# A convolution and a greedy sparse code of 16 images: one coefficient tile in four rebuilt from dictionary rows, and written-out orders for both ends

## The chip, the cores and the metric

One core of one Trainium2 chip runs the kernel. The metric is the device time of one execution in microseconds, the median of the runs.

## The reference

The input `x` is (16, 64, 128, 128), f32. Two layers stand one behind the other, each a residual step on a group norm with 32 groups:

```python
x = x + _L0_conv_ref(_gn(x), L0_conv_weight)
x = x + _L1_conv_ref(_gn(x), L1_conv_dictionary)
```

The first is a circular 3x3 convolution with 64 channels in and out (written with an FFT). The second cuts an image into 4x4 patches over all channels, 1024 numbers each (1024 patches an image), and codes each patch by five greedy steps of orthogonal matching pursuit on a dictionary of 512 normalised words of 1024:

```python
for k in range(1, K_MAX + 1):
    scores = jnp.abs(h * (~mask).astype(h.dtype))
    index = jnp.argmax(scores, axis=1).astype(jnp.int32)
    ...
    x_stack = jax.scipy.linalg.solve_triangular(jnp.swapaxes(L, -1, -2), y, lower=False)[..., 0]
    beta = jnp.einsum('bk,bkn->bn', x_stack, G[I])
    h = h_bar - beta
coeffs = jnp.zeros((B, N), X.dtype).at[bidx[:, None], I].set(x_stack)
```

`G` is the Gram matrix of the words, `h_bar` the correlations of a patch with all 512. The patch that goes out is the dictionary times `coeffs`, a sum of five weighted words.

## The kernel before

**Tiles.** A tile is 128 patches on the partitions (`h`: 512 correlations each). An image has 8, in two groups of T = 4. SyncE loads rows of the image (`xh` for the convolution, `xs` for the statistics) and stores `xa`, the result of the first layer. Per image TensorE does eight rounds of `convolve` (`conv_ps`), eight of `correlate` (16 matmul instructions of 512 columns into one of three banks `gen_ps`, from `z`, the normalised patches, and `dn`, the words), `turn` for each tile and sixteen of `recon`. ScalarE evacuates: `ev` writes `xa`, `z` makes the patches, `h` copies correlations, `ct` copies turned coefficients, `re` copies reconstructed rows to `rb`; `st` and `rt` are the group norm's statistics.

**The pursuit.** A unit (back, g, k) is step k of group g of image i - back. ScalarE writes absolute values (`score`, L625), VectorE finds the largest and its place (`search`, L763 and L772) and the word's index and, for k > 0, the addresses of the cells of the Gram matrix between it and the k words before (`cell`, L781). GpSimd then gathers, one instruction for a cell or a row of each tile: `v` (L476, 4k instructions of 128 numbers) and for k < 4 the word's Gram row (`u`, L489, 4 instructions of 128 rows of 2 KB). VectorE turns the cells into a row of the inverse factor (`factor_row`), orthogonalises the Gram row against the kept ones (`project`, L872) and takes it off `h` (L880). The two groups alternate, so that one's gathers lie beside the other's search: UNITS is the order of the ten units of a period.

**The reconstruction.** After k = 4 `coefficients` (`co`) solves for the five weights `xc`. `ce` builds the dense 128 x 512 coefficients of a tile on VectorE: the first word by one instruction (L668), the other four by a mark `hot` where a count equals the index (L658) and an addition of weight times mark (L674), for two tiles at a time in alternation. `turn` transposes it by four 128x128 matmuls (L926) into `ct`, and `recon` multiplies 4 tiles, 512 columns, by the transposed words `dt`:

```python
for a in range(NA):
    last = pe.matmul(to[:], dt_[:, a, d, :], ct[:, g % CT_RING, a, :], start=(a == 0), stop=(a == NA - 1))
```

Four of these 16 blocks of an image make a quarter in `rb`, of which there are two in turn, and GpSimd adds it to the output in memory (`add`, L497).

**Order.** All engines run in program order. Period i holds the convolution of image i, most of the pursuit of image i - 1, and the reconstruction of image i - 2. VECTOR_PLAN, SCALAR_PLAN and ADD_PLAN say at which point of which unit each piece of other work is put on VectorE, ScalarE and GpSimd; BANKS which of three banks a `correlate` or `recon` uses; `period` of TensorE is written out by hand. The first periods use the same tables with the parts left out whose image doesn't exist; the closing one (i = 16) has tables of its own (TAIL...).

## Time and profile before

| | |
|---|---|
| Median of 3 runs | 3405.57 us (3388.78 to 3411.45) |
| Profiled execution, its own time | 3407.99 us |
| Its span, first to last instruction | 3406.1 us |
| Mean granted TensorE clock | 0.953 |
| TensorE / VectorE / ScalarE / GpSimd busy | 88% / 79% / 50% / 58% |

A period in the middle begins with a search of group 0 of a new image. Busy time of TensorE is near to what it can do only when its granted clock is 1.00, and busy time of GpSimd leaves out the time in which it prepares the next transfer, which the waits list as "issue". The rows that matter follow behind the change.

### The profile page before, as it was taken

What the parts mean: (1) busy time and instruction counts of PE and PEld (TensorE: products, weight loads), DVE (VectorE), ACT (ScalarE), POOL (GpSimd) and SP (SyncE); (2) the same over time, 40 slices, a digit from 0 to 9 for tenths busy, and PEclk for the clock granted to TensorE, in tenths of its full rate; (3) what the DMA queues carried; (4) which work ended last, traced back from release to release, by engine and by line L of the source; (5) the groups of instructions that cost most, each with busy time, mean ns of one, the idle gap of its engine ahead of it and who ended that gap; (6) DMA issues with size and microseconds to landing.
All of it is one profiled execution on the core that took longest, in us unless ns stands there. A gap on an engine that the chain in (4) does not pass through costs nothing.

```text
span 3406.1 us, 33931 instructions
## 1 busy us (share of the span) xinstructions
PE 3012.6 (88%) x9424; PEld 1276.3 (37%) x9424; DVE 2681.5 (79%) x6981; ACT 1717.0 (50%) x2899; POOL 1989.0 (58%) x1869
## 2 busy tenths in 40 slices
PE   4996899899999999999999999999999999995547
PEld 1342334343434444343434434343443434342223
DVE  1137888888888888888888888888888878888883
ACT  4545454564646455464646546464645546442222
POOL 0025576656656666666656556665666676666562
PEclk9997999999999999999999999999999999997778
DMA  3433344443454444344454444445444434432133
GB/s 137 144 115 121 132 133 114 162 126 128 114 164 146 140 130 128 122 126 141 146 157 134 112 146 111 134 140 157 140 113 156 126 121 120 140 106 66 47 74 62
DMA packets 139148, 428.32 MB, mean 126 GB/s; under 512 B 56656, under 2 KB 56912, under 8 KB 121936
## 3 DMA queue, kind: packets, MB, share of 16 engines
q0 software_dynamic: 91776, 204.20, 23.9%
q1 hardware_dynamic: 47184, 221.96, 18.1%
q8 instruction: 76, 1.25, 0.1%
q14 instruction: 112, 0.92, 0.1%
HBM read 289.70 MB, written 136.31 MB: 125 GB/s over the span
## 4 chain that ended last, share of the span: by engine, by line
PE 33%; POOL 23%; DVE 17%; issue 11%; DMA 10%; ACT 4%; ACTq 0%; POOLq 0%; DVEq 0%
POOL v L476 20%; PE gen_ps L967 14%; PE gen_ps L955 10%; DMA u<-marked_rows,chosen 9%; DVE u L872 5%; PE conv_ps L1023 4%; DVE idx L772 4%; DVE top L763 3%; POOL u L489 2%; PE conv_ps L1030 2%; DVE h L880 2%; ACT score L625 1%; DVE ce L674 1%; ACT z L553 1%; PE gen_ps L984 1%
## 5 line engine op out<-in xcount | busy, mean ns | idle before, releaser
L476 POOL DMA_INDIRECT v<-gram_rows,cell x1280 | 1386.3, 1083 | 861.2 <-DVE cell L781 496.8
L955 PE MATMUL gen_ps<-ct,dt 128*128 128x512 f32 x2048 | 943.4, 617 | 67.3 <-ACT rb L541 44.4
L967 PE MATMUL gen_ps<-dn,z 128*128 128x512 f32 x2048 | 915.2, 600 | 27.1 <-ACT z L553 24.0
L1023 PE MATMUL conv_ps<-xh,wc 128*128 128x512 f32 x1536 | 711.0, 613 | 81.1 <-ACT xa L576 80.0
L625 ACT ACTIVATE score<-h 128x512 f32<-128x512 f32 x640 | 379.9, 604 | 726.0 <-DVE top L763 375.8
L489 POOL DMA_INDIRECT u<-marked_rows,chosen x504 | 526.4, 1044 | 230.0 <-issue 149.5
L955 PEld LDWEIGHTS gen_ps<-ct,dt 128*128 128x128 f32 x2048 | 396.9, 198 | 560.5 <-issue 528.9
L967 PEld LDWEIGHTS gen_ps<-dn,z 128*128 128x128 f32 x2048 | 385.7, 192 | 530.9 <-issue 492.0
L872 DVE SCALAR_TENSOR_TENSOR u<-u,nl 128x512 f32<-128x512 f32 x748 | 515.8, 748 | 82.3 <-DMA u<-marked_rows,chosen 79.1
L763 DVE MAX8 top<-score 128x8 f32<-128x512 f32 x640 | 417.7, 690 | 201.8 <-ACT score L625 183.0
L1023 PEld LDWEIGHTS conv_ps<-xh,wc 128*128 128x128 f32 x1536 | 294.1, 195 | 457.9 <-issue 456.8
L772 DVE FIND_INDEX8 idx<-h 128x8 uint32<-128x520 f32 x640 | 432.1, 694 | 0.0
L880 DVE SCALAR_TENSOR_TENSOR h<-u,na,h 128x512 f32<-128x512 f32 x504 | 355.7, 747 | 49.2 <-DMA u<-marked_rows,chosen 48.5
L541 ACT ACTIVATE rb<-gen_ps 128x512 f32<-128x512 f32 x256 | 275.9, 1106 | 223.6 <-PE gen_ps L955 222.0
L674 DVE SCALAR_TENSOR_TENSOR ce<-hot,xc,ce 128x512 f32<-128x512 f16 x512 | 359.3, 741 | 0.0
L1032 PE MATMUL conv_ps<-xh,wq 64*64 64x512 f32 x1536 | 359.2, 597 | 0.0
L1030 PE MATMUL conv_ps<-xh,wq 64*64 64x512 f32 x1536 | 359.2, 597 | 0.0
L553 ACT ACTIVATE z<-xa,fac 128x512 f32<-128x512 f32 x256 | 290.3, 1258 | 39.3 <-PE gen_ps L967 39.3
L576 ACT ACTIVATE xa<-conv_ps,shift 128x1024 f32<-128x1024 f32 x128 | 140.8, 1100 | 278.5 <-PE conv_ps L1032 278.5
L926 PE MATMUL ct_ps<-ident,ce 128*128 128x128 f32 x512 | 85.8, 293 | 143.2 <-DVE ce L674 74.6
L1030 PEld LDWEIGHTS conv_ps<-xh,wq 64*64 64x64 f32 x1536 | 102.0, 131 | 238.4 <-issue 238.4
L530 ACT ACTIVATE ct<-ct_ps 128x512 f32<-128x512 f32 x128 | 76.2, 595 | 196.3 <-PE ct_ps L926 196.3
(110 smaller groups left out, 1819.3 us busy)
## 6 DMA issues: line engine op xcount, KB each, us to landing
xh<-x_paired SPq DMA_DIRECT2D x128, 650.0 KB, 4.9
y_rows<-xa SPq DMA_DIRECT2D x64, 1024.0 KB, 5.2
y_rows<-rb POOLq DMA_DIRECT2D x64, 1024.0 KB, 8.8
xs<-x_pairs SPq DMA_DIRECT2D x120, 512.0 KB, 3.8
v<-gram_rows,cell POOLq DMA_INDIRECT x1280, 2.4
u<-marked_rows,chosen POOLq DMA_INDIRECT x504, 4.5
xa<-x_pairs SPq DMA_DIRECT2D x4, 1024.0 KB, 7.9
dn<-atoms SPq DMA_DIRECT2D x1, 2048.0 KB, 11.6
```

What stands on the lines that cost most here:

```text
L476: pool.indirect_dma_start(v[:, g, k - 1, j, t:t + 1], None, cells, bass.IndirectOffsetOnAxis(ap=cell[:, g, k // (KMAX - 1), j, t:t + 1], a ...
L489: pool.indirect_dma_start(kept(img, g, k, t), None, marked, bass.IndirectOffsetOnAxis(ap=chosen[:, g, t:t + 1], axis=0))\
L625: act.activation(score[t % 2][:], h[:, g * T + t, 0:ATOMS], ACT.Abs).then_inc(score_ready[g], 1)
L674: dve.scalar_tensor_tensor(ce[:, place, :], hot[:, m % HOT_RING, :], coef, ce[:, place, :], ALU.mult, ALU.add).then_inc(ce_step, 1)
L763: dve.max(top8[:, t, :], score[t % 2][:]).then_inc(top_found[g], 1)
L772: dve.max_index(idx8[:, t, :], h[:, g * T + t, ATOMS:HW], h[:, g * T + t, :]).then_inc(located[g], 1)
L872: dve.scalar_tensor_tensor(kept(img, g, k, t), kept(img, g, j, t), nl[:, g, k - 1, j, t:t + 1], kept(img, g, k, t), ALU.mult, ALU.add).the ...
L880: dve.scalar_tensor_tensor(hh, kept(img, g, k, t), na[:, g, k, t:t + 1], hh, ALU.mult, ALU.add)\
L955: last = pe.matmul(to[:], dt_[:, a, d, :], ct[:, g % CT_RING, a, :], start=(a == 0), stop=(a == NA - 1))
L967: last = pe.matmul(to[:], z[:, t % 2, d // PATCH, d % PATCH, :], dn[:, d, :], start=(d == 0), stop=(d == ND - 1))
L1023: pe.matmul(conv_ps[:, a], wc[:, tap, a * CIN:a * CIN + P], rows[:, a + 1:a + 2 * CP:2, tap:tap + W], start=(tap == 0), stop=False)
L1030: pe.matmul(conv_ps[above, a], wq[second, tap, :], rows[second, a:a + 2 * CP - 1:2, tap:tap + W], start=False, stop=(tap == TAPS - 1))
```

## The change

1. **Three tiles in four are multiplied (TURNED = 3).** `ce`, `turn` and `ct` leave the fourth tile out; `recon` has 384 columns in place of 512. For the fourth tile, `fetch` gathers the five chosen words themselves, 128 rows of 4 KB each, from a new table in memory (`atom_rows`, written once by SyncE from `dt` after image 1). ScalarE scales the first by its weight (`ps`), VectorE adds the other four (`pk`, 1024 columns each), and TensorE transposes a 128x128 part of the sum into the last 128 columns of each block's bank. Two buffers hold the sums, two the fetched words, so a fetch of word 3 or 4 waits for the addition two before it. `coefficients` ends with a copy of the indices (`pick`).
2. **One outgoing buffer (RB_RING = 1)** in place of two: the first `re` of each quarter waits until the quarter before has been added in memory.
3. **Orders.** The first three images and the last two have an order of their own on every engine (HEAD, TAIL with 18 and 32 units; with the 11 periods between them, 160 units as before). In the middle, group 1's coefficients and reconstruction come a period later (image i - 3); weights and indices of four images are kept (CO_RING). The loads of `xs` are spread over more rounds.
4. **The last group of the last image** reads its cells on the chip for k > 1 (`read_cells`): VectorE multiplies a mark with the kept rows and sums; GpSimd gathers only the first cell of each tile, and the elimination in `factor_row` falls away.

The core of the diff:

```diff
+HEAD_IMAGES = 3
+TAIL_IMAGES = 2
+CO_RING = 4
...
-CE_RING = 4
+TURNED = T - 1
+CE_RING = TURNED
+ROWS_RING = 4
 XS_RING = 2
-RB_RING = 2
+RB_RING = 1
...
-    0: [0, 1, 2], 5: [3, 4], 7: [5, 6, 7],
+    0: [0, 1], 1: [2], 2: [3, 4, 5], 3: [6], 5: [7],
...
+HEAD = ((3, 0, 0), (3, 0, 1), (3, 0, 2), (3, 1, 0), (3, 0, 3), (3, 1, 1), (3, 0, 4), (3, 1, 2), (2, 0, 0), (3, 1, 3),
...
+TAIL = ((3, 0, 0), (4, 1, 3), (3, 0, 1), (4, 1, 4), (3, 0, 2), (3, 1, 0), (3, 0, 3), (3, 1, 1), (3, 0, 4), (3, 1, 2),
...
+VECTOR_PLAN = {
+    1: [(3, ("ce", 1, 0))], 1.5: [(2, ("co", 0))], 11.5: [(3, ("pk", 1, 3)), (3, ("pk", 1, 4)), (3, ("ce", 1, 1))],
+    21: [(2, ("ce", 0, 0))], 24: [(2, ("pk", 0, 1)), (2, ("pk", 0, 2))],
...
+ADD_PLAN = {
+    0: [(3, ("get", 1, 4)), (2, ("get", 0, 0))], 2: [(2, ("get", 0, 1)), (2, ("get", 0, 2))],
+    5: [(3, ("add", 1, 0)), (2, ("get", 0, 3)), (2, ("get", 0, 4))], 6: [(3, ("add", 1, 1)), (2, ("get", 1, 0))],
+    7: [(2, ("get", 1, 1)), (2, ("add", 0, 0)), (2, ("get", 1, 2))], 9: [(2, ("get", 1, 3)), (2, ("add", 0, 1))],
+}
...
+                if i == 1:
+                    sp.wait_ge(turned_copied, 2 * NA)
+                    sp.dma_start(words.rearrange("(a p) (d c) -> p a d c", p=P, c=P), dt_[:]).then_inc(rows_out, 16)
...
-                        for j in range(k):
+                        for j in range(1 if read_in_place(img, g, k) else k):
...
+            def fetch(img, g, j):
+
+                n = img * GROUPS + g
+                if j == 0:
+                    pool.wait_ge(pick_ready, n + 1)
+                    if n == 0:
+                        pool.wait_ge(rows_out, 16)
+                    if n > 1:
+                        pool.wait_ge(recon_done, (n - 1) * ND)
+                elif n > 0 or j > 2:
+                    pool.wait_ge(atom_step, n * (KMAX - 1) + j - 2)
+                place, _ = atom_load(n, j)
+                pool.indirect_dma_start(atom[:, place, :], None, words,
+                                        bass.IndirectOffsetOnAxis(ap=pick[:, img % CO_RING, g, j:j + 1], axis=0))\
+                    .then_inc(atom_loaded[place], 16)
...
+                elif kind == "ps":
+
+                    g, = a
+                    n = img * GROUPS + g
+                    act.wait_ge(solve_step, solved(img, g))
+                    act.wait_ge(atom_loaded[n % 2], 16 * atom_load(n, 0)[1])
+                    act.activation(atom[:, n % 2, :], atom[:, n % 2, :], ACT.Copy,
+                                   scale=xc[:, img % CO_RING, g, 0, TURNED:T]).then_inc(atom_scaled, 1)
...
+                    members = (0, 1) if pair == 0 else (2,)
...
+                elif kind == "pk":
+
+                    g, j = a
+                    n = img * GROUPS + g
+                    own = n % 2
+                    other, loads = atom_load(n, j)
+                    dve.wait_ge(atom_loaded[other], 16 * loads)
+                    if j == 1:
+                        dve.wait_ge(atom_scaled, n + 1)
+                    else:
+                        dve.wait_ge(atom_step, n * (KMAX - 1) + j - 1)
+                    dve.scalar_tensor_tensor(atom[:, own, :], atom[:, other, :], xc[:, img % CO_RING, g, j, TURNED:T],
+                                             atom[:, own, :], ALU.mult, ALU.add).then_inc(atom_step, 1)
...
+            def read_cells(img, g, k):
+
+                dve.wait_ge(which_ready[g], at(img, KMAX, k + 1))
+                dve.wait_ge(row_step[g], at(img, ROWS, T * sum(range(k))))
+                for j in range(1, k):
+                    for t in range(T):
+                        m = T * sum(range(1, k - 1)) + (j - 1) * T + t
+                        if m:
+                            dve.wait_ge(cell_read, m)
+                        dve.scalar_tensor_tensor(hot[:, 0, :], count[:], which[:, img % CO_RING, g, k, t:t + 1],
+                                                 kept(img, g, j, t), ALU.is_equal, ALU.mult,
+                                                 accum_out=v[:, g, k - 1, j, t:t + 1]).then_inc(cell_read, 1)
+                dve.wait_ge(cell_read, T * sum(range(1, k)))
...
+            def recon(img, g, d):
+
+                pe.wait_ge(ct_ready, at(img, GROUPS * TURNED, (g + 1) * TURNED))
+                if d == 0:
+                    pe.wait_ge(atom_step, (img * GROUPS + g + 1) * (KMAX - 1))
+                m = bank_of(img, images, ("re", g, d))
+                room(m, recon_out, at(img, GROUPS * ND, g * ND + d + 1))
+                to = gen_ps[m]
                 for a in range(NA):
-                    last = pe.matmul(to[:], dt_[:, a, d, :], ct[:, g % CT_RING, a, :], start=(a == 0), stop=(a == NA - 1))
...
+                    pe.matmul(to[:, 0:TURNED * P], dt_[:, a, d, :], ct[:, g % CT_RING, a, :], start=(a == 0), stop=(a == NA - 1))
+                own = (img * GROUPS + g) % 2
+                pe.transpose(to[:, TURNED * P:], atom[:, own, d * P:(d + 1) * P], ident[:]).then_inc(recon_done, 1)
```

TensorE, a whole period in the middle, from the last blocks of one group's reconstruction to the first correlations of the image (L955/L1178 are `recon`, L1180 the new transposes, L926/L1160 `turn`, L967/L1192 `correlate`; x counts equal instructions in a row). Before:

```order
L955 MATMUL gen_ps<-ct,dt 128x512 x12
L926 MATMUL ct_ps<-ident,ce 128x128 x4
L955 MATMUL gen_ps<-ct,dt 128x512 x4
L1004 MATMUL conv_ps<-mv,avg 128x5
L926 MATMUL ct_ps<-ident,ce 128x128 x8
L955 MATMUL gen_ps<-ct,dt 128x512 x16
L967 MATMUL gen_ps<-dn,z 128x512 x8
L955 MATMUL gen_ps<-ct,dt 128x512 x4
L967 MATMUL gen_ps<-dn,z 128x512 x8
L1004 MATMUL conv_ps<-mv,avg 128x5
```

In the change:

```order
L1229 MATMUL conv_ps<-mv,avg 128x5
L1160 MATMUL ct_ps<-ident,ce 128x128 x4
L1229 MATMUL conv_ps<-mv,avg 128x5
L1178 MATMUL gen_ps<-ct,dt 128x384 x4
L1180 MATMUL gen_ps<-ident,atom 128x128
L1178 MATMUL gen_ps<-ct,dt 128x384 x4
L1180 MATMUL gen_ps<-ident,atom 128x128
L1178 MATMUL gen_ps<-ct,dt 128x384 x4
L1180 MATMUL gen_ps<-ident,atom 128x128
L1234 MATMUL conv_ps<-fac,tap_sum 128x1
L1178 MATMUL gen_ps<-ct,dt 128x384 x4
L1180 MATMUL gen_ps<-ident,atom 128x128
```

A block is now four matmuls (two instructions each) of 384 columns and one transpose; the averages of the group norm move ahead of the reconstruction's second half.

GpSimd, from the gathers of the last two units of a period to those of the fourth and fifth of the next (`v` are cells, `u` Gram rows, `atom` the fetched words, `y_rows` the additions). Before:

```order
L476 DMA v<-gram_rows,cell 128x1 x24
L489 DMA u<-marked_rows,chosen 128x512 x4
L497 DMA y_rows<-rb 128x2048 x2
L489 DMA u<-marked_rows,chosen 128x512 x4
L476 DMA v<-gram_rows,cell 128x1 x12
L489 DMA u<-marked_rows,chosen 128x512 x4
L476 DMA v<-gram_rows,cell 128x1 x4
L489 DMA u<-marked_rows,chosen 128x512 x4
L476 DMA v<-gram_rows,cell 128x1 x24
```

In the change:

```order
L660 DMA v<-gram_rows,cell 128x1 x24
L673 DMA u<-marked_rows,chosen 128x512 x4
L696 DMA atom<-atom_rows,pick 128x1024
L681 DMA y_rows<-rb 128x2048
L673 DMA u<-marked_rows,chosen 128x512 x4
L696 DMA atom<-atom_rows,pick 128x1024 x2
L660 DMA v<-gram_rows,cell 128x1 x12
L673 DMA u<-marked_rows,chosen 128x512 x4
L660 DMA v<-gram_rows,cell 128x1 x4
L673 DMA u<-marked_rows,chosen 128x512 x4
L696 DMA atom<-atom_rows,pick 128x1024 x2
L660 DMA v<-gram_rows,cell 128x1 x24
```

Five of a period's ten fetches stand here, each between one unit's gathers and the next one's; the additions stand apart.

VectorE, the end of the program, between the last search and the last solve (`ce` and `hot` belong to group 0, `tmp_last` to `sq_last` to the last solve of group 1). Before, behind nine rows of group 0's tiles:

```order
L658 TENSOR_SCALAR hot<-count,which 128x512 x2
L674 SCALAR_TENSOR_TENSOR ce<-hot,xc,ce 128x512 x2
L794 TENSOR_TENSOR tmp_last<-nl,v 128x12
L797 TENSOR_TENSOR v<-v,tmp_last 128x12
L794 TENSOR_TENSOR tmp_last<-nl,v 128x8
L797 TENSOR_TENSOR v<-v,tmp_last 128x8
L794 TENSOR_TENSOR tmp_last<-nl,v 128x4
L797 TENSOR_TENSOR v<-v,tmp_last 128x4
L801 SCALAR_TENSOR_TENSOR nl<-v,rd 128x16
L805 TENSOR_TENSOR sq_last<-nl,v 128x16
```

In the change:

```order
L996 SCALAR_TENSOR_TENSOR cell<-which 128x16
L1000 SCALAR_TENSOR_TENSOR hsel<-pos,top 128x4
L889 SCALAR_TENSOR_TENSOR atom<-atom,xc 128x1024 x2
L1013 SCALAR_TENSOR_TENSOR hot,v<-count,which,u 128x512 x4
L1013 SCALAR_TENSOR_TENSOR hot,v<-count,which,xs 128x512 x4
L1013 SCALAR_TENSOR_TENSOR hot,v<-count,which,xh 128x512 x4
L1030 SCALAR_TENSOR_TENSOR nl<-v,rd 128x16
L1034 TENSOR_TENSOR sq_last<-nl,v 128x16
L1038 TENSOR_REDUCE ss_last<-sq_last 128x4
```

Twelve reads on the chip stand in place of the six steps of elimination, and no tile of group 0 is left behind the last search.

## Rows read from the trace of the kernel before

**Rows 1.** The page: shares (1) and 40 slices (2)
```profile
PE 3012.6 (88%) x9424; PEld 1276.3 (37%) x9424; DVE 2681.5 (79%) x6981; ACT 1717.0 (50%) x2899; POOL 1989.0 (58%) x1869
...
PE   4996899899999999999999999999999999995547
...
DVE  1137888888888888888888888888888878888883
```

**Rows 2.** Timeline, VectorE: start us, us, line, operation, tiles [idle before]
```profile
550.35 1.30 DVE L763 MAX8 top<-score 128x8 f32<-128x512 f32 x2 [0.54 <-ACT score L625]
...
3098.56 1.30 DVE L763 MAX8 top<-score 128x8 f32<-128x512 f32 x2 [0.83 <-ACT score L625]
```

**Rows 3.** Windows: us; busy PE, PEld, DVE, ACT, POOL (count); clock; DMA share, GB/s
```profile
178.90:550.40 371.50, 318.64 (x1038) 134.07 (x1037) 269.86 (x713) 192.04 (x337) 204.70 (x194) 0.93 0.38 121
550.40:2703.20 2152.80, 2029.23 (x6404) 858.10 (x6403) 1827.17 (x4775) 1170.41 (x1981) 1367.65 (x1277) 0.98 0.45 135
2703.20:3098.60 395.40, 371.09 (x1162) 156.73 (x1160) 329.47 (x858) 192.26 (x315) 258.60 (x234) 0.97 0.41 120
3098.60:3273.60 175.00, 77.80 (x180) 35.07 (x180) 160.43 (x399) 49.06 (x72) 107.34 (x108) 0.74 0.30 75
3273.60:3364.20 90.60, 55.03 (x130) 25.25 (x131) 65.41 (x176) 19.10 (x24) 42.89 (x44) 0.77 0.24 47
3364.20:3406.10 41.90, 28.75 (x72) 12.64 (x70) 0.04 (x1) 10.86 (x11) 2.53 (x3) 0.89 0.42 75
```

**Rows 4.** Groups by line, 550.4 to 2703.2: count, busy us, mean ns, idle before
```profile
L955 PE MATMUL gen_ps<-ct,dt 128*128 128x512 f32 x1408 | 646.5, 615 | 48.3 <-ACT rb L541 33.3 <-ACT ct L530 15.1
...
L926 PE MATMUL ct_ps<-ident,ce 128*128 128x128 f32 x352 | 56.2, 283 | 18.9 <-DVE ce L674 10.4 <-ACT ct L530 8.6
...
L872 DVE SCALAR_TENSOR_TENSOR u<-u,nl 128x512 f32<-128x512 f32 x528 | 364.2, 748 | 57.2 <-DMA u<-marked_rows,chosen 54.8
...
L674 DVE SCALAR_TENSOR_TENSOR ce<-hot,xc,ce 128x512 f32<-128x512 f16 x352 | 247.0, 741 | 0.0
L658 DVE TENSOR_SCALAR hot<-count,which 128x512 f16<-128x512 f16 x352 | 108.4, 348 | 0.0
L668 DVE TENSOR_SCALAR ce<-count,which,xc 128x512 f32<-128x512 f16 x88 | 46.0, 565 | 0.4
...
L785 DVE SCALAR_TENSOR_TENSOR hsel<-pos,top 128x4 f32<-128x4 f32 x110 | 18.1, 165 | 0.8
...
L476 POOL DMA_INDIRECT v<-gram_rows,cell x880 | 962.5, 1094 | 559.4 <-DVE cell L781 308.6 <-issue 250.8
L489 POOL DMA_INDIRECT u<-marked_rows,chosen x353 | 362.5, 1027 | 135.5 <-issue 105.1 <-DVE chosen L777 30.4
```

**Rows 5.** Waits, 550.4 to 2703.2: us in total, times, longest
```profile
DVE top L763 <- ACT score L625: 107.2, 59, 5.2
...
POOL y_rows L497 <- ACT rb L541: 90.6, 11, 9.7
...
DVE tmp L794 <- DMA v<-gram_rows,cell: 50.6, 13, 5.0
...
DVE h L880 <- DMA u<-marked_rows,chosen: 27.7, 26, 2.5
...
DVE tmp_last L794 <- DMA v<-gram_rows,cell: 16.6, 19, 2.4
```

**Rows 6.** The page, DMA issues: count, KB each, us to landing
```profile
y_rows<-rb POOLq DMA_DIRECT2D x64, 1024.0 KB, 8.8
...
v<-gram_rows,cell POOLq DMA_INDIRECT x1280, 2.4
u<-marked_rows,chosen POOLq DMA_INDIRECT x504, 4.5
```

**Rows 7.** Timeline of the end, TensorE, VectorE
```profile
3366.68 27.73 PE L955 MATMUL gen_ps<-ct,dt 128*128 128x512 f32 x64 [0.69 <-ACT ct L530]
...
3343.23 0.17 DVE L794 TENSOR_TENSOR tmp_last<-nl,v 128x12 f32<-128x12 f32 x1 [13.58 <-DMA v<-gram_rows,cell]
```

More of the change, by code:

```diff
@@ L169, in units, with bank_of @@
-def units(i, images):
-    return TAIL if i == images else UNITS
-def planned(plan, tail, last, place):
-    return tail.get(place, ()) if last else [(lag(what), what) for what in plan.get(place, ())]
-def bank_of(back, what, last):
-    return [((back, what) if last else what) in bank for bank in (TAIL_BANKS if last else BANKS)].index(True)
+)
+def bank_of(img, images, what):
+    if img < images and any((HEAD_IMAGES - img, what) in bank for bank in HEAD_BANKS):
+        return [(HEAD_IMAGES - img, what) in bank for bank in HEAD_BANKS].index(True)
+    if any((images - img, what) in bank for bank in TAIL_BANKS):
+        return [(images - img, what) in bank for bank in TAIL_BANKS].index(True)
+    return [what in bank for bank in BANKS].index(True)
@@ L498, in add, with period @@
                     .then_inc(recon_added[(g * PHASES + ph) % RB_RING], 16)
[L500 to L506 removed]
+            def fetch(img, g, j):
[12 more added lines that the diff above has]
+                    .then_inc(atom_loaded[place], 16)
+            def period(i, order, plan):
+                for n, (back, g, k) in enumerate(order):
+                    gather(i - back, g, k)
+                    for b, (kind, *what) in plan.get(n, ()):
+                        if kind == "add":
                             add(i - b, *what)
+                        else:
+                            fetch(i - b, *what)
             for a in range(NA):
@@ L603, in root, with period @@
                 act.activation(gs[:, 2:3], gs[:, 1:2], ACT.Sqrt, bias=eps[:, 0:1]).then_inc(gn_root[n], 1)
-            def period(i, par):
-                here = parts(i)
-                for n, (back, g, k) in enumerate(units(i, images)):
+            def period(i, order, plan):
+                for b, what in plan.get(-1, ()):
+                    extra(what, i - b)
+                for n, (back, g, k) in enumerate(order):
                     img = i - back
-                    if here[back]:
-                        scored.append((img, g, k))
+                    scored.append((img, g, k))
@@ L949, in recon, with room @@
[L949 to L960 removed]
+            def room(m, taken, count):
+                if m in free:
+                    pe.wait_ge(*free[m])
+                free[m] = (taken, count)
```

702 lines of the change are left out of this document (417 added, 285 removed), and 163 rows, old and new, of tables (BANKS, HEAD_SCALAR_PLAN, HEAD_VECTOR_PLAN, SCALAR_PLAN).

## The prediction

> **What bounds the kernel now.** I read the page's engine shares first, then its slices [rows 1]. TensorE is busy 88% of the span, VectorE 79%, GpSimd 58%; TensorE's slices are nearly all 9 from the third to the thirty-sixth, but open with 4 and close with 5547. VectorE's slices are the reverse: 1, 1, 3 at the start and 8 until the last. So the run has three parts, and I cut it where VectorE begins its first search (178.88), the first search of period 3 (550.35), of period 14 (2703.18) and of the closing period 16 (3098.56); two of these starts stand in [rows 2], the others are read in the same way. The stretches between them give the table on which everything below rests [rows 3]: a start of 178.9, a head of 371.5, eleven whole periods in 2152.8 (195.7 each), and a tail of 702.9 us.
>
> In one of the eleven periods TensorE is busy 2029.23 / 11 = 184.5 us (94%) and VectorE 1827.17 / 11 = 166.1 (85%). GpSimd's busy time is 1367.65 / 11 = 124.3, but its queue takes more: before most gathers come 0.3 us of "issue" in which it can do nothing else, 250.8 + 105.1 us in all [rows 4], so the queue is taken (1367.65 + 355.9) / 11 = 156.7 us (80%). TensorE is the bound here. VectorE idles 29.6 us a period; its largest named waits [rows 4, 5] are for scores, 107.2 / 11 = 9.7 us (ScalarE, which stands in its queue behind evacuations of matmuls), and for gathered rows and cells, (54.8 + 50.6 + 27.7 + 16.6) / 11 = 13.6.
>
> From 3098.6 to 3273.6 ten units are searched with TensorE only 44% busy; VectorE is busy 160.43 of 175.0 us, 92% [rows 3]. That stretch shows how close VectorE comes to its own floor with this order of units when TensorE doesn't hold it, and it is my measure for the changed kernel.
>
> **The change part by part: one period.** TensorE: the 128 matmul instructions of the reconstruction go from 512 to 384 columns. They are busy 646.5 / 11 = 58.8 us a period [rows 4], so a quarter less is -14.7. Two of eight tiles are no longer turned: 8 transposes at 56.2 / 352 = 0.16 are -1.3. Sixteen transposes of a word are new, +2.6 at the same 0.16. Net -13.4, TensorE 171.1. That time follows columns down to 384 is not shown here; the turns take 0.16 at 128 columns, a quarter of the width and 35% of the 0.459 (646.5 / 1408) of a 512-column one, so the saving on a quarter lies between 0.22 x 58.8 = 12.7 and 14.7. I take the upper, since the busy time of a turn holds the filling of a lone group of four, which a long row of blocks pays once.
>
> VectorE: a coefficient tile costs 4 x (247.0 + 108.4) / 352 + 46.0 / 88 = 4.56 us [rows 4]; two fewer are -9.1. Eight additions of 1024 columns are new. No row has this shape. One of 512 columns lasts 748 ns and one of 4 columns 165 [rows 4], a slope of 1.15 ns a column, so 748 + 512 x 1.15 = 1.34 us each; bounds are 1.2 (twice the 0.69 busy of one, less a shared start) and 1.5 (twice 748). That is +10.7. Two copies of the picked indices are +0.3. The third tile now stands alone, so its marks and additions no longer alternate with a partner's: eight steps with some 0.15 of uncovered latency, +1.2, bounds 0 and 3. Net +3.1, VectorE 169.
>
> GpSimd: ten fetches of 512 KB. A row gather is busy 362.5 / 353 = 1.03 us and comes with 0.3 of issue [rows 4], so +13.3, and the queue is taken 170 us. Their landing: a gather of cells lands 2.4 us after its issue, one of 256 KB after 4.5 [rows 6], so by the slope 512 KB after 6.6; bounds 4.5 and 9. What is queued behind a fetch is the next gather, for which VectorE waits; the queue idles (308.6 + 30.4) / 11 = 31 us a period for VectorE's indices [rows 4], and that idle time takes most of the ten.
>
> The Trainium skill, "DMA: Bandwidth & Descriptors", section on the anatomy of one DMA on the SWDGE path, gives 2.0 us plus the bytes at 436 GB/s, which would be 3.2 us for 512 KB. The trace disagrees at 256 KB: 4.5 us against 2.6 by the page. By its figure the fetches would be cheaper, and no term of the sum would change.
>
> ScalarE: one scaling of 1024 columns per group for one copy of 512, about +1 us on an engine 54% busy. Nothing. A single buffer for the outgoing rows is a new wait: the next quarter's first copy waits for the previous addition to land, 8.8 us after its issue [rows 6], and behind that copy stand the scores. I give it no term of its own beyond the share taken below, since the copies of two quarters now have a whole search between them in the plan; see the rivals for what it costs uncovered.
>
> The sum of a period: the floors are TensorE 171, VectorE 169, GpSimd 170. None alone fills 9 parts in 10 of the present 195.7. VectorE needs 169 / 0.92 = 184 at the share it reaches unhindered; at its present 85% it would need 199. With TensorE freed but two other queues fuller I take 90%, so 188. Eleven periods: 11 x (195.7 - 188) = -85, between 11 x 11.7 = -129 and about -10.
>
> TensorE's clock: the granted clock is 0.98 in the periods at 94% busy, 0.93 in the head at 86%, 0.74 at 44% [rows 3]. At 171 of 188 (91%) I expect about 0.96, which makes 171 into 175: still under 188, so nothing.
>
> The Trainium skill, "TensorE: Matmul & The Clock Gate", Part 1, says that the clock is halved when the array has been idle and given back when it has been busy, which speaks against any saving on TensorE. These rows agree with its direction; it costs nothing as long as TensorE isn't the last to finish.
>
> **The head.** It is written out on its own now, and the second group's coefficient tiles of the first image leave it. VectorE's 269.9 us lose 8 tiles (36.5) and get 3 tiles and 6 additions (13.7 + 8.0): 255. TensorE loses half of a reconstruction. Its share now is 73%, since in the first units one group alone goes from search to gather to search. I take 77.5%: 329 us, -42; bounds -15 and -65.
>
> **The tail.** VectorE is busy 329.47 + 160.43 + 65.41 = 555.3 us from 2703.2 to 3364.2 (84%) [rows 3]. Added: 4 images x 3.1 = 12; the delayed group's 3 tiles and 2 additions, 16.4; and 24 reads of cells on the chip at 364.2 / 528 = 0.69, 16.6, less a dozen tiny operations (2). About 598. What the reads remove: the last solve waits 13.58 us for sixteen gathers [rows 7], and twelve reads (8.3) with four gathers beside them take their place; that shows in the share. With the conv work spread over the tail's whole length I take 90%: 664 against 661, +3. Then the last eight blocks: 27.73 us of matmuls [rows 7] become 20.8 + 1.3, -5.6; but the last word's fetches go through two buffers, so I add 3 for the fourth and fifth. The tail comes to 0; bounds -40 and +30.
>
> Sum against the profiled execution's own 3408.0 (span 3406.1; the median of the runs is 3405.6, so both agree to 0.1%): -85 - 42 + 0 = -127, **3281 us**.
>
> **The rivals.** First, the pursuit's chain through GpSimd is already the floor. For it: 13.6 us of waits for gathered data a period although TensorE bounds, a queue 80% taken, and gathers of one group that take up to (962.5 + 250.8) / 880 x 16 = 22 us [rows 4] in front of the other group's. Against it: the 175 us stretch, with the same order of units and 14.6 us of idle VectorE in all [rows 3]. Then ten fetches cost their 13 us and a period comes to 194; head -30: 3408 - 19 - 30 = 3359. 
>
> Second, it goes better: the separate orders for the ends and the deeper lag keep VectorE at 92% everywhere. Period 184, head 315, tail -25: 3408 - 129 - 56 - 25 = 3198.
>
> Third, slower: the single outgoing buffer. Four times a period ScalarE can stand for the addition's issue and 8.8 us of landing, some 40 us; TensorE's three banks fill behind it and VectorE's scores stand behind it. It is uncovered when the copy of the next quarter comes less than 10 us after the last one's. Every microsecond exposed costs 11 on the total; from 11.5 a period all of the gain is gone, and with 15 exposed (37%) a period is 203: 3408 + 80 - 42 + 4 = 3450. For it: GpSimd already waits 90.6 us in the eleven periods until a quarter is copied, with two buffers [rows 5]. Against it: ScalarE is idle 46% of the time, and the four additions are spread over the period.
>
> **Chances.** Forecast 0.50; gather chain 0.18; better 0.22; single buffer 0.10. A measurement of this kernel can tell about 1%, 34 us. The forecast and the better case are faster by more; of the gather chain 0.09 is and the rest within 1%; of the single buffer 0.08 is slower. Faster 0.81, same 0.11, slower 0.08. The range: from the better case's 3198 to a little over the gather chain's 3359, 3195 to 3380; below it 0.08 is left, above 0.12.
>
> **What would show it.** Periods between searches of 184 to 192 us; the reconstruction's instructions at 0.75 of their busy time; additions of 1024 columns at 1.2 to 1.5 us; the ends of VectorE's and TensorE's shares near 90%. Wrong: VectorE waiting over 20 us a period for gathers (first rival), or ScalarE or TensorE waiting over 10 us a period for an outgoing copy (third); a head over 355 us, or a tail over 730.

## The result, and the profile after

The changed kernel takes 3287.77 us, the median of 4 runs (3283.51 to 3298.51), against 3404.97 us (3388.78 to 3411.45) for the kernel before: a ratio of 0.967, 95% interval 0.963 to 0.971. The forecast was 3281. The profiled execution took 3298.51 us by its own time, with a span of 3296.2. Below, ratios and intervals leave out executions in a slower state of the chip; one of an experiment's own runs was such a one, in experiment 11, where the median without it is 3303.09 us.

Cut at the same searches as [rows 3], the windows of the changed kernel (columns as there: stretch, its length, busy time of TensorE, its weight loads, VectorE, ScalarE and GpSimd, granted clock, DMA share, GB/s) are:

```profile
0.00:178.40 178.40, 131.49 (x442) 53.93 (x442) 28.94 (x64) 85.62 (x165) 5.28 (x13) 1.00 0.37 134
178.40:513.40 335.00, 287.62 (x969) 123.10 (x970) 257.17 (x677) 182.62 (x324) 199.36 (x195) 0.93 0.45 149
513.40:2577.00 2063.60, 1897.75 (x6495) 868.35 (x6494) 1858.49 (x4697) 1178.15 (x1981) 1417.23 (x1390) 0.97 0.57 169
2577.00:3212.00 635.00, 458.76 (x1484) 219.26 (x1482) 549.74 (x1365) 258.43 (x403) 426.55 (x394) 0.86 0.46 130
3212.00:3258.30 46.30, 31.86 (x94) 18.10 (x93) 39.26 (x92) 15.61 (x18) 14.91 (x12) 0.85 0.56 132
3258.30:3296.20 37.90, 22.29 (x74) 12.65 (x72) 0.00 (x0) 9.03 (x9) 2.71 (x3) 0.90 0.46 83
```

The head went from 371.5 to 335.0 us (-36.5), the eleven periods from 2152.8 to 2063.6 (-89.2; 187.6 each, where they were 195.7), and the tail from 702.9 to 719.2 (+16.3). With -0.5 at the start that is -109.9 on the span. In a period TensorE is now busy 1897.75 / 11 = 172.5 us (92%) and VectorE 1858.49 / 11 = 169.0 (90%).

The groups by line, in the eleven periods, that answer to [rows 4] (L1178 is `recon`, L1180 the turn of the word's sum, L889 the addition, L696 the fetch):

```profile
L1178 PE MATMUL gen_ps<-ct,dt 128*128 128x384 f32 x1408 | 509.2, 510 | 21.9 <-ACT rb L749 20.6
L889 DVE SCALAR_TENSOR_TENSOR atom<-atom,xc 128x1024 f32<-128x1024 f32 x88 | 112.7, 1280 | 2.8 <-DVE atom L889 0.5
L696 POOL DMA_INDIRECT atom<-atom_rows,pick x110 | 111.1, 1010 | 33.5 <-issue 33.5
L1180 PE MATMUL gen_ps<-ident,atom 128*128 128x128 f32 x176 | 48.0, 273 | 0.0
```

The reconstruction's busy time is 509.2 where it was 646.5, -12.5 us a period: 0.79 of it, for 0.75 of the columns. This ratio and the 48.0 us of the turns must be read with care, because the records of neighbouring instructions of TensorE overlap. The timeline of two blocks shows the distance from start to start:

```profile
1005.42 2.75 PE L1178 MATMUL gen_ps<-ct,dt 128*128 128x384 f32 x8
1008.00 0.27 PE L1180 MATMUL gen_ps<-ident,atom 128*128 128x128 f32 x1
1008.11 2.75 PE L1178 MATMUL gen_ps<-ct,dt 128*128 128x384 f32 x8
```

Eight instructions of 384 columns take 1008.00 - 1005.42 = 2.58 us, 0.32 each, and the turn takes 0.11 until the next block starts, though its record is 0.27 long. The 64 instructions of 512 columns in 27.73 us [rows 7] come to 0.43 each. By this measure the time does follow the columns (0.32 / 0.43 = 0.75), and sixteen turns put back some 1.8 us a period and not 48.0 / 11 = 4.4. All products into `gen_ps` together, correlations and turns included, are busy 1128.45 us in the eleven periods where they were 1263.18, -12.2 a period.

And the waits of the same stretch, which answer to [rows 5] (columns: engine, what waits, what ended the wait, us in total, times, longest):

```profile
ACT rb L749 <- DMA y_rows<-rb: 140.7, 21, 9.6
DVE top L978 <- ACT score L830: 93.2, 67, 3.4
PE conv_ps L1229 <- DVE fac L912: 61.6, 11, 7.2
POOL y_rows L681 <- ACT rb L749: 39.8, 20, 4.4
PE conv_ps L1248 <- DMA xh<-x_paired: 37.4, 11, 5.2
DVE h L1116 <- DMA u<-marked_rows,chosen: 21.2, 12, 2.8
DVE tmp L1023 <- DMA v<-gram_rows,cell: 13.7, 10, 2.4
DVE u L1108 <- DMA u<-marked_rows,chosen: 6.9, 10, 2.2
DVE tmp_last L1023 <- DMA v<-gram_rows,cell: 3.1, 4, 1.3
```

VectorE's waits for gathered data are (21.2 + 13.7 + 6.9 + 3.1) / 11 = 4.1 us a period, a third of what they were, though ten larger transfers now pass through the same queue. New are ScalarE's wait for the outgoing buffer, 140.7 / 11 = 12.8, and two waits of TensorE: 5.6 for VectorE's step of the statistics and 3.4 for the convolution's rows. They look like the next things to remove. Experiments 8, 10 and 12 tried the two of TensorE, and it brought nothing.

### The profile page after: what moved, and what is told of

The parts are those of the page before. It is cut to its first block, busy times and chain, and to the rows that moved or that the text cites. A ratio compares the mean times of both kernels' runs of the same rounds, so it can differ in the third digit from the quotient of the medians.

```text
span 3296.2 us, 34238 instructions
## 1 busy us (share of the span) xinstructions
PE 2829.8 (86%) x9552; PEld 1295.4 (39%) x9552; DVE 2733.6 (83%) x6889; ACT 1729.5 (52%) x2899; POOL 2066.0 (63%) x2005
## 4 chain that ended last, share of the span: by engine, by line
PE 28%; DVE 22%; POOL 21%; DMA 11%; issue 11%; ACT 5%; SPq 0%; ACTq 0%; POOLq 0%; DVEq 0%
POOL v L660 18%; PE gen_ps L1192 11%; PE gen_ps L1178 7%; DVE u L1108 6%; PE conv_ps L1248 5%; DVE idx L987 5%; DMA y_rows<-rb 4%; DMA u<-marked_rows,chosen 4%; DVE top L978 3%; POOL u L673 3%; DVE h L1116 2%; PE conv_ps L1255 2%; DMA xh<-x_paired 2%; ACT score L830 2%; DMA v<-gram_rows,cell 1%
## 5 line engine op out<-in xcount | busy, mean ns | idle before, releaser
L660 POOL DMA_INDIRECT v<-gram_rows,cell x1256 | 1307.8, 1041 | 706.5 <-issue 362.1
L1192 PE MATMUL gen_ps<-dn,z 128*128 128x512 f32 x2048 | 912.8, 600 | 28.4 <-ACT z L761 23.1
L1178 PE MATMUL gen_ps<-ct,dt 128*128 128x384 f32 x2048 | 751.8, 516 | 100.1 <-ACT rb L749 80.0
L1248 PE MATMUL conv_ps<-xh,wc 128*128 128x512 f32 x1536 | 720.7, 620 | 106.1 <-ACT xa L783 64.1
L673 POOL DMA_INDIRECT u<-marked_rows,chosen x504 | 515.3, 1022 | 186.1 <-issue 153.2
L1192 PEld LDWEIGHTS gen_ps<-dn,z 128*128 128x128 f32 x2048 | 384.3, 192 | 514.6 <-issue 488.1
L1178 PEld LDWEIGHTS gen_ps<-ct,dt 128*128 128x128 f32 x2048 | 395.5, 202 | 394.6 <-issue 202.4
L876 DVE SCALAR_TENSOR_TENSOR ce<-hot,xc,ce 128x512 f32<-128x512 f16 x384 | 275.9, 744 | 4.5
L696 POOL DMA_INDIRECT atom<-atom_rows,pick x160 | 165.0, 1031 | 91.4 <-issue 46.0
L889 DVE SCALAR_TENSOR_TENSOR atom<-atom,xc 128x1024 f32<-128x1024 f32 x128 | 163.8, 1280 | 13.6 <-DMA atom<-atom_rows,pick 9.7
```

The source lines that it names most:

```text
L660: pool.indirect_dma_start(v[:, g, k - 1, j, t:t + 1], None, cells, bass.IndirectOffsetOnAxis(ap=cell[:, g, k // (KMAX - 1), j, t:t + 1], a ...
L673: pool.indirect_dma_start(kept(img, g, k, t), None, marked, bass.IndirectOffsetOnAxis(ap=chosen[:, g, t:t + 1], axis=0))\
L1178: pe.matmul(to[:, 0:TURNED * P], dt_[:, a, d, :], ct[:, g % CT_RING, a, :], start=(a == 0), stop=(a == NA - 1))
L1192: last = pe.matmul(to[:], z[:, t % 2, d // PATCH, d % PATCH, :], dn[:, d, :], start=(d == 0), stop=(d == ND - 1))
L1248: pe.matmul(conv_ps[:, a], wc[:, tap, a * CIN:a * CIN + P], rows[:, a + 1:a + 2 * CP:2, tap:tap + W], start=(tap == 0), stop=False)
```

## The experiments

The first four ran on a chip on which the kernel before took 4018 us, the others on chips on which it took 3399 to 3409. So every result is given by its ratio to the kernel before, run beside it on the same chip (the changed kernel has 0.967), and stretches are compared among the traces of the second kind alone. "Head", "period" and "tail" are cut as above.

**Experiments 1 and 5: the orders alone.** All four tiles are multiplied again, in the changed kernel's orders and with its one outgoing buffer; fetches, scaling, additions and the turn of the sum are gone.

```diff
-TURNED = T - 1
+TURNED = T
-                    members = (0, 1) if pair == 0 else (2,)
+                    members = (0, 1) if pair == 0 else (2, 3)
...
-                    pe.matmul(to[:, 0:TURNED * P], dt_[:, a, d, :], ct[:, g % CT_RING, a, :], start=(a == 0), stop=(a == NA - 1))
+                    last = pe.matmul(to[:], dt_[:, a, d, :], ct[:, g % CT_RING, a, :], start=(a == 0), stop=(a == NA - 1))
```

> The changed kernel's orders (its plans, its own orders for head and tail, its bank tables, its last cells read on chip, one outgoing buffer), but all four tiles multiplied, so no dictionary rows fetched, scaled, added or turned. My theory, that the rebuilt tile carries most of the gain in the middle (TensorE's own work per period 184.5 -> 172.5) and the orders most of the gain in the head: TensorE's work is back at about 185 a period, the period at 193 to 196, the time 3340 to 3390. Rival, that the orders carry it all: period 188 to 190, time 3290 to 3315, and the rebuilt tile is worth nothing. Second rival, that the single outgoing buffer costs in this order: period over 197, time over 3400.

Measured on the first chip: 4201.54 us, 1.044 of before (1.039 to 1.049).

> The same kernel as the first experiment (the changed kernel's orders, four tiles multiplied, one outgoing buffer), run again, because the kernel before itself took 4018 us on the chip of those runs and 3405 on the chip of the first comparison. My theory, that the rebuilt tile carries the gain of the middle and the orders that of the head: on a chip where the kernel before takes about 3405, a period of 193 to 196 and 3340 to 3390 us in all. Rival, that the orders carry it all: period 188 to 190, 3290 to 3315 us. Second rival, the single outgoing buffer: period over 197, over 3400 us.

Measured: 3434.83 us, 1.010 (1.0085 to 1.0118). Its windows, with the end of VectorE's work as the last cut:

```profile
178.21:511.42 333.21, 292.42 (x963) 122.23 (x964) 253.61 (x678) 181.31 (x323) 195.10 (x186) 0.93 0.39 130
511.42:2694.70 2183.28, 2026.89 (x6404) 860.09 (x6403) 1837.68 (x4794) 1175.42 (x1981) 1320.29 (x1279) 0.97 0.46 133
2694.70:3372.02 677.32, 521.80 (x1527) 226.14 (x1525) 579.95 (x1485) 269.71 (x419) 385.99 (x366) 0.90 0.37 98
```

The head is 333.2, as short as in the changed kernel, so the head's gain of 37 belongs to the orders. The period is 198.5: 2.8 longer than before, with TensorE at 184.3. From here to the changed kernel the period falls by 10.9, with 11.8 us less work for TensorE and 1.9 us more for VectorE. The tail (677.3 + 53.5) is 730.8, 28 longer than before. So orders, single buffer and the reads on the chip together cost 1%, and the rebuilt tile, put into these orders, is worth 1 - 0.967 / 1.010 = 4.3%. The rebuilt tile in the old orders wasn't run. The period was over my range and the total was where the rival of the single buffer had it, though this run doesn't say that the buffer is the reason.

**Experiment 2: two buffers in the new orders.**

```diff
-RB_RING = 1
+RB_RING = 2
```

(on experiment 1, whose memory has room for it; the changed kernel's has not).

> As the run before it (the changed kernel's orders, four tiles multiplied), with two outgoing buffers again. It prices the single buffer in the new orders. My theory: the wait for the outgoing transfer (12.8 us a period on ScalarE in the changed kernel) hides behind ScalarE's free time, so within 10 us of the run with one buffer. Rival, that it is paid in part: 20 to 60 us faster than with one buffer (2 to 5 us a period).

Measured: 4212.22 us, 1.047 (1.042 to 1.051), the same as with one. In the new orders the second buffer is worth nothing there. This was seen on the first chip alone, where a period of either kernel is near 256 us and not 198.5, so it doesn't show that the second buffer would be worth nothing on the others.

**Experiments 3 and 9: one buffer in the old orders.** The kernel before with `RB_RING = 1` for 2.

> The kernel before with one outgoing buffer in place of two and nothing else. My theory as in the prediction: the wait on ScalarE is below what it has to spare, so 0 to +25 us (0 to 2 a period), 3405 to 3430. Rival of the prediction (the buffer as the bound): more than 11.5 us a period uncovered, so over 3500 us.

Measured on the first chip: 4727.34 us, 1.174 (1.168 to 1.180).

> The kernel before with one outgoing buffer instead of two, run again on another chip than at first (there the kernel before took 4018 us and this one 4727). My theory as in the prediction: below what ScalarE has to spare, 3405 to 3430. Rival 3 of the prediction: over 11.5 us a period uncovered, over 3530.

Measured: 4112.27 us, 1.209 (1.204 to 1.215). My theory is wrong by some 700 us and the prediction's rival right, for this order. The timeline of ScalarE (start, length, line, tile, idle time before it and what ended it) shows the wait, and GpSimd's shows its cause:

```profile
1502.23 1.07 ACT L541 ACTIVATE rb<-gen_ps 128x512 f32<-128x512 f32 x1
...
1553.02 1.07 ACT L541 ACTIVATE rb<-gen_ps 128x512 f32<-128x512 f32 x1 [31.53 <-DMA y_rows<-rb]
```

and on GpSimd:

```profile
1508.83 1.05 POOL L476 DMA_INDIRECT v<-gram_rows,cell  x1 [24.22 <-DVE cell L781]
1510.19 1.00 POOL L476 DMA_INDIRECT v<-gram_rows,cell  x1 [0.30 <-issue]
...
1543.24 0.96 POOL L489 DMA_INDIRECT u<-marked_rows,chosen  x1 [0.30 <-issue]
1544.20 1.05 POOL L497 DMA_DIRECT2D y_rows<-rb  x1
...
1567.98 0.90 POOL L497 DMA_DIRECT2D y_rows<-rb  x1 [22.73 <-ACT rb L541]
```

The quarter was complete at 1503.3. Its addition stood behind 28 gathers in GpSimd's order and was issued at 1544.2, 41 us later; it landed 8.8 us after that, and only then could ScalarE go on. Then GpSimd stood at the next addition for 22.73 us until the next quarter was copied, with the gathers behind it. So ScalarE and GpSimd wait for each other in turn. In the changed kernel the same pair of views shows on ScalarE:

```profile
1019.08 1.96 ACT L749 ACTIVATE rb<-gen_ps 128x512 f32<-128x512 f32 x2
1032.96 3.00 ACT L749 ACTIVATE rb<-gen_ps 128x512 f32<-128x512 f32 x3 [9.06 <-DMA y_rows<-rb]
```

and on GpSimd:

```profile
1023.73 1.02 POOL L681 DMA_DIRECT2D y_rows<-rb  x1
1039.31 1.00 POOL L681 DMA_DIRECT2D y_rows<-rb  x1 [1.43 <-ACT rb L749]
```

Complete at 1021.0, issued at 1023.7, landed 9.2 us later. With one buffer in both, the delay before the issue is 41 us here and 2.7 there, so the price of a single buffer seems to go with the place of the addition. This is read from two traces: no run moved the additions alone. If it is so, the change could give up the buffer, and use its memory for the words of the fourth tile, only together with ADD_PLAN's new places.

**Experiment 6: no fetches.** The entries ("get", ...) leave ADD_PLAN and its relatives, and `atom` is filled with zeros once; the waits for a landed fetch go. The run leaves out the fourth tile's words, so that tile's output lacks its dictionary part.

```diff
-                    dve.wait_ge(atom_loaded[other], 16 * loads)
...
-                    act.wait_ge(atom_loaded[n % 2], 16 * atom_load(n, 0)[1])
+                    act.wait_ge(atom_filled, 1)
```

> The changed kernel without its 160 fetches of dictionary rows: the scaling on ScalarE, the additions on VectorE and the turning on TensorE run as before on a buffer that is filled with zeros once. Left out: the words of the fourth tile, so that tile's output lacks its dictionary part. It prices the queue and the landing alone (10 fetches a period, 13 us of GpSimd's 165). My theory: the gathers have slack (VectorE waited 4.1 us a period for them), so 0 to -3 us a period, 3250 to 3288. Rival 1 of the prediction (GpSimd's chain is the floor): -8 or more a period, under 3200.

Measured: 3271.77 us, 0.962 (0.959 to 0.9645). Period 185.8 (-1.8), tail 716.3 (-2.9). Ten transfers of 512 KB a period and 13 us of GpSimd's queue are nearly free, as I expected: room in GpSimd's queue is not what sets the period. The gathers themselves stayed, so this run says nothing of their own price.

**Experiment 7: no additions.** The entries ("pk", ...) and ("ps", ...) leave the plans, the fetches stay. The run leaves out the weighted sum: TensorE turns the first fetched word as it is. ScalarE also has 2 us a period less to do.

```diff
-                    pe.wait_ge(atom_step, (img * GROUPS + g + 1) * (KMAX - 1))
+                    pe.wait_ge(atom_loaded[(img * GROUPS + g) % 2], 16 * ((img * GROUPS + g) // 2 + 1))
```

> The changed kernel without the scaling and the 128 additions of the fourth tile's words; the 160 fetches stay, and TensorE turns the first fetched row unscaled. Left out: the sum over the five atoms of the fourth tile. It takes 10.2 us a period from VectorE (169 of 187.6) and 4.1 from ScalarE. My theory (VectorE with 90% of the period is what bounds it, TensorE with 172.5 close behind): -5 to -9 us a period, 3190 to 3235. Rival, that TensorE or the queue bounds it: 0 to -2, 3265 to 3288.

Measured: 3235.39 us, 0.950 (0.948 to 0.953). The total lies just above my range (3190 to 3235), but not for my reason:

```profile
510.49:2550.20 2039.71, 1888.17 (x6486) 864.85 (x6487) 1750.58 (x4610) 1156.07 (x1959) 1391.55 (x1390) 0.97 0.57 171
2550.20:3188.32 638.12, 476.85 (x1550) 229.70 (x1548) 548.06 (x1421) 262.53 (x410) 416.43 (x407) 0.88 0.48 137
```

The period lost 9.8 us of VectorE's work (169.0 to 159.1) and became 2.2 us shorter (185.4), about what experiment 6 gained; experiment 11 has the changed kernel's very periods and shows 186.9, so a good half microsecond of this is the difference between two executions. So VectorE's work is not what sets the length of a period. The tail lost 40.9 us of VectorE's work (589.0 to 548.1) and 33.4 us of time (719.2 to 685.8): there most of the work that goes comes back as time.

**Experiments 8, 10 and 12: three ways to take a wait from TensorE.** Experiment 8 moves the product for which TensorE waited 5.6 us behind two blocks of the reconstruction:

```diff
-                average(i + 1, 0)
                 recon(i - 2, 0, 0)
                 recon(i - 2, 0, 1)
+                average(i + 1, 0)
```

> The changed kernel with one line moved in TensorE's order of a period: the small product for the next image's statistics behind the first two reconstruction blocks rather than ahead of them. It waits 5.6 us a period for VectorE's step of the statistics there. My theory: two blocks (4.6 us) slide into that wait, TensorE has the more slack, and since VectorE is the tighter one, 0 to -2 us a period: 3265 to 3288. Rival, that TensorE's queue sets the period: -4 to -5 a period, about 3235. Rival the other way: the statistics then come late and the next convolution waits, +2 or more a period, over 3310.

Measured: 3312.15 us, 0.973 (0.970 to 0.975). The median is where the second rival had it (over 3310); the interval still touches the changed kernel's (0.963 to 0.971), so a small loss is at the edge of what these runs can tell; no gain is seen. Period 188.5. The wait of 61.6 us is gone from the eleven periods, and waits of `recon` have come up, 88.8 us where there were 20.6:

```profile
PE gen_ps L1178 <- ACT rb L749: 49.7, 12, 5.5
PE gen_ps L1178 <- ACT ct L731: 39.1, 11, 4.7
```

TensorE's idle time of a period is 15.1 us, as before the move: it was shifted to another place and not taken away.

Experiment 10 lets VectorE do its step earlier (also at two places of the tail, not shown) and sends a chunk later:

```diff
-    30: [(0, ("gn", 1, 1))], 32.5:
+    29.5: [(0, ("gn", 1, 1))], 32.5:
...
-    0: [0, 1], 1: [2], 2: [3, 4, 5], 3: [6], 5: [7],
+    0: [0, 1], 1: [2], 2: [3, 4], 3: [5, 6], 5: [7],
```

> The changed kernel with two moves aimed at TensorE's two largest waits of a period. First, VectorE's step of the second statistics goes ahead of the four maxima instead of behind them (it ran 3.8 us after its input was there, in each period, and TensorE waited 5.6 for it); in the tail the same step of the last two images likewise (13 and 9 us late). Second, SyncE sends the sixth chunk of the next image behind the outgoing rows rather than ahead of them, where it held the next rows back until TensorE waited 3.4 us. Nothing is left out and no work added. After the runs without fetches and without additions, which moved the period by only 2 us each, my theory is that VectorE and TensorE hand work to each other and both waits are partly paid: -1 to -3 us a period and up to -5 in the tail, 3245 to 3275. Rival, that TensorE's waits are paid in full: -6 a period, 3215 to 3225. Rival the other way, as with the later average: a move shifts the wait elsewhere, 3285 to 3310.

Measured: 3318.76 us, 0.973 (0.970 to 0.976), again a little above the changed kernel and at the edge of what can be told. The wait for the convolution's rows (37.4) has vanished from the eleven periods, but the wait at L1229, which the first move was for, has not: 62.1 us. The period is 188.8; the head is 343.1, 8 longer.

> The first of the two moves of the tenth experiment alone: VectorE's step of the second statistics ahead of the four maxima instead of behind them in each period, and likewise at two places of the tail; SyncE's chunks as in the changed kernel. With both moves the time was 3319 us: 9 us more in the head, 6 in the first period, about 1 in each further one. My theory: the chunk that SyncE sent later cost that (ScalarE's sums of the next image came late), and this move alone is neutral: 3275 to 3295. Rival: the statistics ahead of the maxima cost it, since ScalarE's next scores wait for the maxima: 3300 to 3320.

Measured for the first move alone: 3303.07 us, 0.972 (0.970 to 0.974), by the ratio half a per cent above the changed kernel, with intervals that overlap. Its waits of TensorE in the eleven periods:

```profile
PE gen_ps L1178 <- ACT rb L749: 34.0, 12, 4.5
PE conv_ps L1248 <- DMA xh<-x_paired: 32.0, 11, 5.3
PE conv_ps L1229 <- DVE fac L912: 29.1, 11, 4.0
...
PE gen_ps L1178 <- ACT ct L731: 15.5, 11, 1.4
```

The wait at L1229 fell from 61.6 to 29.1, 3.0 us a period, and the period stayed 187.6 to the tenth. Of these 32.5 us, 28.9 stand again in `recon`'s waits for ScalarE's copies (34.0 + 15.5, where there were 20.6 and none): here too the wait went to another place. The head is 336.4, so the longer head of experiment 10 came with the chunk. The total is in the rival's range, but its trace doesn't show the rival's cost: head +1.4, eleven periods +0.3, tail +2.

**Experiments 4 and 11: the last cells gathered.**

```diff
-            return img == images - 1 and g == GROUPS - 1 and k > 1
+            return False
```

> The changed kernel with the last group's cells gathered through the queue again instead of read on chip by VectorE (24 reads of 0.79 us = 19 us of VectorE work go; 36 gathers come back in their place). My theory: the last solve waits some 13.6 us for its gathers as it did before, where the twelve reads took 9.5, and the earlier blocks save what their reads took while other work stood by: between 0 and +8 us, 3288 to 3296. Rival, that the reads cost VectorE more than the wait: 3 to 10 us faster, 3278 to 3285.

Measured on the first chip: 4025.62 us, 1.002 (0.999 to 1.005). The changed kernel itself wasn't run there.

> The changed kernel with the last group's cells gathered instead of read on chip, run again on another chip than at first (where the kernel before took 4018 us). My theory: 0 to +8 us against the changed kernel's 3288 or so. Rival, that the reads cost VectorE more than the wait they replace: 3 to 10 us faster, 3278 to 3285.

24 gathers come back (the page counts 1280 of cells for 1256), not the 36 that I had expected. Measured: 3307.71 us, 0.971 (0.967 to 0.974), which by itself can't be told from the changed kernel. The traces can be: up to the last unit the tails are the same (633.8 and 635.0 us), from there to the end it is 97.7 us with gathers and 84.2 with reads. VectorE's last solve stands in the timelines of the two, with gathers:

```profile
3231.34 0.17 DVE L1023 TENSOR_TENSOR tmp_last<-nl,v 128x12 f32<-128x12 f32 x1 [19.90 <-DMA v<-gram_rows,cell]
```

and in the changed kernel with reads, the first and the last of twelve:

```profile
3222.22 0.75 DVE L1013 SCALAR_TENSOR_TENSOR hot<-count,which,u 128x512 f16<-128x512 f16 x1
3222.89 0.08 DVE L1013 DVE_READ_ACCUMULATOR hot<-count,which,u 128x1 f32 x1
...
3231.64 0.08 DVE L1013 DVE_READ_ACCUMULATOR hot<-count,which,xh 128x1 f32 x1
```

Twelve reads take 9.5 us where the gathers left VectorE idle for 19.9. The reads are worth some 13 us at the end, more than my 0 to 8.

## Why the prediction was right, and where it was off

The forecast was 127 us less; the span of the profiled execution fell by 109.9, and the median, 3287.77 us, lies inside the range. The head fell short of it by 5.5 us and the tail by 16.3, the periods gave 4.2 more. The sums of the engines' work came out; the step from work to the length of a period did not, as said below, and there the number was met by luck.

**Start and head.** Head 335.0 for a predicted 329: VectorE's work came to 257.2 for 255, and its share to 76.8% for 77.5%. Experiment 5 shows that this gain is the orders' own.

**The work of a period.** VectorE 169.0 us for 169, with an addition at 1.28 for 1.34. TensorE 172.5 for 171.1. Reconstruction and turns were to give 14.7 - 2.6 = 12.1, and the products into `gen_ps` gave 12.2. The busy time of the reconstruction alone seems to give only the lower end (12.5 for 12.7), but from start to start its time followed the columns, as I had argued; the turns cost some 1.8 us and not the 4.4 of their records. The 1.4 us missing are for the most part the convolution and the averages (492.8 and 10.7 us in the eleven periods, for 487.6 and 6.3), to which I gave nothing. On VectorE the 0.15 us for each step of the tile that stands alone, for which I had no row, is borne out: a mark and an addition were busy 355.4 / 352 = 1.01 us and are 283.3 / 268 = 1.06, which is +1.1 a period for 1.2. GpSimd's queue is taken (1417.23 + 255.7 + 107.5 + 33.5) / 11 = 164.9 for 170. A fetch lands 7.8 us after its issue; I had 6.6, between 4.5 and 9.

**The length of a period.** 187.6 for 188, but the step to it, a VectorE that fills 90% of the time and thereby bounds it, isn't how the period works. I took a share between two that the old profile had (85% and 92%); it met the result, but as a cause it fell, since experiment 7 took 9.8 us of work from VectorE and shortened the period by 2.2. Experiment 6 freed GpSimd's queue and gained 1.8.

What the period does follow in these runs is TensorE's work, which I had as no longer the bound. In the eight traces of the new orders on the chips of the second kind (the changed kernel and experiments 5 to 8 and 10 to 12) a period is 13.8 to 16.2 us longer than TensorE's busy time, whether that is 184.3 (experiment 5) or 171.1 (experiment 6), and whether VectorE is busy 159.1 or 169.3. From experiment 5 to the changed kernel TensorE lost 11.8 us and the period 10.9, though VectorE and GpSimd had more to do. TensorE's work of 172.5 at the 92.8% that it fills in experiment 5 would make 185.9. No run took work from TensorE alone, so this stands as the reading that fits all eight, and what the 15 us of its idle time hang on stays open: experiments 8 and 12 only moved them from one wait to another.

**The tail.** The term that was mis-sized: 0 predicted, +16.3 measured. The work was less than I said (589.0 us for 598) and the share was 86.5% where I took 90%; 598 / 0.9 was 664, and 589.0 / 0.865 is 681. I took the share from what I hoped the spread convolutions would do. The shares at hand say otherwise: 84% before, 85.6% in experiment 5, 86.5% in the changed kernel and 85.9% in experiment 7 (82.8% in experiment 11, where VectorE waits for the last gathers). In the tail the time goes roughly with VectorE's work, as experiment 7 shows, and the delayed group brings work there. The last stretch without VectorE is 37.9 us for 41.9, -4.0 where my two terms made -2.6.

**The rivals.** The gather chain as the floor (3359) is refuted at the price that it gave the fetches, 13 us a period: VectorE waits 4.1 us for gathered data, and experiment 6 gained 1.8. The single buffer (3450) is real, and was put too mildly: in the old orders it costs 21% (experiment 9), because I counted only the landing of 8.8 us and not the addition's place behind 28 gathers. I gave it 0.10 as I saw the additions "spread over the period"; by the traces it matters more that each stands close behind its last copy. My sign for this rival, over 10 us a period of waiting for an outgoing copy, came up in the changed kernel (12.8 on ScalarE) while the period was as forecast, so that sign was badly chosen: what of this wait reaches the period wasn't measured on a chip of the second kind. The better case (3198) failed on the head (335.0 for 315), the period (187.6 for 184) and the tail (+16 for -25).

**No version that is faster than both** came out of these runs: the three edits that left the computation whole and aimed at TensorE's waits (experiments 8, 10 and 12) have 0.972 or 0.973 of before, the changed kernel 0.967, with intervals that just meet.

## What to carry to other kernels

When two engines are both near nine tenths busy, a wait of either is no gain in store: it can turn up again at the next instruction of the same engine, so add up the engine's whole idle time before and after a move. Leave the work of one engine out, or put it back, and see how much of it comes back in time: here 9.8 us of VectorE's gave 2.2, and 11.8 of TensorE's went with 10.9. Two busy shares side by side don't say which engine sets the time. Before shortening a ring of buffers, look where the instruction that frees the buffer stands on its own engine: what is queued ahead of it, and not its duration alone, can be the price. For the time of one product in a row, take the distance between starts and not the length of a record. Size a draining tail by the busiest engine's work over the share it has in the tail now, and not over the share it has in the steady part.

## What the runs showed that I had not expected

One program takes very different times on two chips. Experiments 1 and 5 are the same kernel: 4201.54 us and 3434.83 (the kernel before: 4018 and 3403). VectorE's work is the same in both (2706.1 and 2700.2 us) and so is GpSimd's (1895.2 and 1909.2); TensorE's is 3120.3 against 3012.5 at a granted clock of 0.87 against 0.954. The chain of waits of the slower one, experiment 1, holds a share by engine that the other has not at all:

```profile
PE 28%; another core or an unknown queue 24%; DVE 19%; issue 13%; ACT 11%; POOL 3%; DMA 1%; ACTq 0%; SPq 0%; POOLq 0%; DVEq 0%
```

and that of experiment 5:

```profile
PE 50%; DVE 18%; POOL 12%; issue 8%; DMA 6%; ACT 5%; SPq 0%; ACTq 0%; POOLq 0%; DVEq 0%
```

What the unknown releaser is wasn't settled. The largest waits without a named one are ScalarE's, 354.8 us before the copies to `ct`, 316.6 before `xa` and 294.2 before `rb`; in experiment 5 the same copies wait for TensorE's products. The rebuilt tile kept its worth there (with the cells gathered, experiment 4 against experiment 1, 4025.62 / 4201.54 = 0.958; here 0.967 / 1.010 = 0.957), and the orders with the single buffer lost 4.4% where they lose 1.0% here.

A gather issued by GpSimd is busy as long for rows of 4 KB (L696, 1.01 us) as for single numbers (L660, 1.02 us, 904.2 us for 883); the size shows only in the landing, 2.4 us, 3.7 for rows of 2 KB (4.5 in the kernel before) and 7.8 for rows of 4 KB (6.0 in experiment 7, 8.4 in experiment 11). And TensorE's instructions start 0.43 us apart at 512 columns, 0.32 at 384 and 0.11 at 128, while their records have 0.79 of the busy time for 0.75 of the columns.
